# A graph network's large node update: the gain of the first norm moved from POOL to DVE's last pass over t

## The chip, the cores and the metric

The kernel runs on one core of one Trainium2 chip. The metric is the device time of one launch in microseconds, median of three runs. One profiled execution of the same program stands beside the runs. The engines are named as in the profile: PE is TensorE (PEld its weight loads), DVE is VectorE, ACT is ScalarE, POOL is GpSimd, SP is SyncE, which here only starts DMAs.

## The reference, cut to what matters

The network has four layers on 50,000 nodes of 64 channels and 25,000 edges: two message layers, one layer with attention over the edges, and a matrix exponential. The change lies in what the third layer does to every node after its attention sums are there:

```python
agg = agg @ Wo + bo
agg = agg * (1.0 + 0.5 * jnp.tanh(gamma))[None, :] + beta[None, :]
x = _layer_norm(node_embeddings + agg, ln1_g, ln1_b)
h = jax.nn.gelu(x @ W1 + b1, approximate=False) @ W2 + b2
return _layer_norm(x + h, ln2_g, ln2_b)

def _layer_norm(x, g, b, eps=1e-05):
    m = jnp.mean(x, axis=-1, keepdims=True)
    v = jnp.mean((x - m) ** 2, axis=-1, keepdims=True)
    return (x - m) * jax.lax.rsqrt(v + eps) * g + b
```

Around it x is normed without weights, clipped at zero and handed to this layer, and the layer's result is added to x; then the next norm follows, whose result the fourth layer reads.

## The kernel before, in words

`node_update` (from line 1421) runs three times, once per layer; the changed branch is `layer == 2`, called the large node update here. It takes the nodes in 14 chunks (`SUPER`) of 128 partitions x 28 rows (`G`) x 64 channels. A tile of a chunk, as `T`, `XC` or `Y`, has 1792 elements in each partition. Each chunk is worked in 7 subchunks (`SUBS`) of 4 rows. Chunks alternate between two buffers `s`. `at(t, d)` names chunk 2t + d.

For each chunk there are two phases, and the engines write out the same order. In the attend phase PE turns the gathered attention rows `A` (`turn`), ACT copies them out of PSUM, PE multiplies by `w_out`, and DVE evacuates each subchunk into T with the layer's input Z added (line 1844). In the MLP phase PE turns T, multiplies by `w1`, ACT applies the gelu with bias `b1`, PE multiplies by `w2`, and DVE evacuates each subchunk, adds it to the gained t and writes Y (line 1846). PE's product of subchunk i + 2 waits for DVE's evacuation of subchunk i, as there are two PSUM buffers. PE runs attend(d) and then mlp(d - 1), in turn.

Between the evacuations DVE works on whole chunks. After T is whole come its row sums (`total`, line 1811), the scaling of `mean` and the centring (`centre`, lines 1815 and 1817), the row sums of ACT's squares (`variance`, line 1821), ACT's root, and then `scale` (lines 1825 and 1830): the reciprocal of the deviation and one tensor_tensor that writes `xc * rstd` over T. This is DVE's last pass over t; it stands in the next chunk's attend phase behind evacuation 1 and raises `t_ready`, for which PE's MLP phase waits. In the same attend phase stand, after evacuation 0, the last pass of an older chunk into H (line 1829), after evacuation 2 the centring of Y, after evacuation 3 the addition of the last bias to X (line 1940), after evacuation 4 the addition of H to X (line 1943), and after evacuation 5 the variance of Y.

The norm's weight and bias `ln1_g` and `ln1_b` aren't applied to T. `prepare` folds them into the MLP: `b1` gets the bias through `w1`, and the rows of `w1` are multiplied by `g1`, the weight as a column (line 266). The sum t + MLP needs t times the weight as well, though; this product is POOL's. `gained` (line 2028) waits for `t_ready` and writes TG = T * `norms[:, 0]` (line 2031), and DVE's first evacuation of the MLP phase waits for `tg_ready`.

POOL's other work is `gather` (line 2033): 28 indirect DMAs for each chunk, 392 in all, each of which fetches one row of 64 channels for every partition into `A` (line 2039). A gather waits until the buffer's last user is through (`inputs_used`). The order on POOL's queue is gather 0, gather 1, and then gained(d), gather(d + 2) for every d.

SP's queue issues all loads and stores; at the start of the program it issues 41 weight loads (line 216), and all engines wait for the last of them.

Of the kernel before, what the change touches and what calls it, by code (L numbers as in the profile page):

```python
# [20 lines left out]
P = 128  # L21
NODES, EDGES, C = 50000, 25000, 64
NH, HD, NET, FF = 4, 16, 8, 128
G = 28
# [106 lines left out]
def prepare(nc, net):  # L131

    d = net.dram
    with ExitStack() as ctx:
        ctx.callback(nc.all_engine_barrier)
        def sb(name, shape, dt=F32):
            return ctx.enter_context(nc.sbuf_tensor(name, shape, dt))
# [5 lines left out]
        bf_row = sb("bf_row", [1, 2 * C])  # L143
        bo_row = sb("bo_row", [1, C])
        wo = sb("wo", [P, C])
        g1 = sb("g1", [P, 1])
        a1 = sb("a1", [C, 1])
        a1_row = sb("a1_row", [1, C])
        rows = sb("rows", [1, 4, C])
# [30 lines left out]
        with nc.Block() as block:  # L180
# [17 lines left out]
                (bf_row[:, :], d["L2_gnn_bf"][None, :]), (bo_row[:, :], d["L2_gnn_bo"][None, :]),  # L198
                (wo[0:C, :], d["L2_gnn_Wo"][:, :]), (wo[C:P, :], d["L2_gnn_Wo"][:, :]),
                (net.w1[0:C, :], d["L2_gnn_W1"][:, :]), (net.w1[C:P, :], d["L2_gnn_W1"][:, :]),  # L200
                (g1[0:C, :], d["L2_gnn_ln1_g"][:, None]), (g1[C:P, :], d["L2_gnn_ln1_g"][:, None]),
                (a1[:, :], d["L2_gnn_ln1_b"][:, None]), (a1_row[:, :], d["L2_gnn_ln1_b"][None, :]),
                (net.b1[:, :], d["L2_gnn_b1"][:, None]),
                (net.w2[:, :], d["L2_gnn_W2"][:, :]), (rows[:, 3, :], d["L2_gnn_b2"][None, :]),
# [36 lines left out]
            def _(v):  # L241
# [21 lines left out]
                nc.vector.tensor_tensor(rows[:, 3, :], rows[:, 3, :], a1_row[:, :], ALU.add)  # L263
                v.wait_ge(up_bias_done, 1)
                nc.vector.tensor_tensor(net.b1[:, :], net.b1[:, :], ps3[:, 0:1], ALU.add)
                nc.vector.tensor_scalar(net.w1[:, :], net.w1[:, :], g1[:, :], None, ALU.mult)
                v.wait_ge(spread_done, 1)
                for half in (slice(0, C), slice(C, P)):
                    nc.vector.tensor_tensor(net.w_out[half, half], wo[half, :], ps2[half, 0:C], ALU.mult)
# [1154 lines left out]
def node_update(nc, net, layer, sums=None):  # L1424
# [19 lines left out]
    with ExitStack() as ctx:  # L1444
# [48 lines left out]
            cols_loaded, rec_ready, scattered = map(sem, ("cols_loaded", "rec_ready", "scattered"))  # L1493
        if layer == 2:
            Y = [sb(f"y{s}", [P, G, C]) for s in range(2)]
            TG = [sb(f"tg{s}", [P, G, C]) for s in range(2)]
            node_end = sb("node_end", [P, SUPER, G])
            ends_loaded = sem("ends_loaded")
            u = [sb(f"u{b}", [FF, 2, CH // 2]) for b in range(2)]

            pf = [ctx.enter_context(nc.psum_tensor(f"{n}pf{b}", [P, 2, 512], F32)) for b in range(2)]
            loaded_x = [sem(f"loaded_x{s}") for s in range(2)]
            gathered = [[sem(f"gathered{s}_{i}") for i in range(SUBS)] for s in range(2)]
            up_done, gelu_done, t_ready, tg_ready, tail_ready = map(
                sem, ("up_done", "gelu_done", "t_ready", "tg_ready", "tail_ready"))
        weight = (net.w_upd, net.w_lin, net.w_out)[layer]
        x_in = (net.x_in, net.x1, net.x2)[layer]
        h_in = (net.h0, net.h1d, net.h2)[layer]
# [9 lines left out]
        def at(t, d):  # L1518

            return 2 * t + d, d % 2, t + d // 2  # L1520
# [9 lines left out]
        with nc.Block() as block:  # L1530
# [271 lines left out]
            def _(v):  # L1802
# [20 lines left out]
                def scale(y, r, n=0, relu=False):  # L1823
# [5 lines left out]
                        return nc.vector.scalar_tensor_tensor(y, XC[n][:, :, :], 0.0, spread(rstd[n][:, :]), ALU.max, ALU.mult)  # L1829
                    return nc.vector.tensor_tensor(y, XC[n][:, :, :], spread(rstd[n][:, :]), ALU.mult)  # L1830

                def evacuate(c, phase, i, m):
                    q, b, s = phase[0] * SUBS + i, (phase[1] + i) % 2, c[1]
                    rows = slice(i * J, (i + 1) * J)
                    got = po[b][:, 0:J * C].rearrange("p (j c) -> p j c", c=C)
                    v.wait_ge(mm_done, q + 1)
                    if layer == 0:
                        to = sums[:, bass.ds(G * c[0] + i * J, J), 0:C]
                        nc.vector.scalar_tensor_tensor(to, got, 0.0, X[s][:, rows, :], ALU.max, ALU.add).then_inc(evacuated, 1)
                    elif layer == 1:  # L1840
                        to = sums[:, bass.ds(G * c[0] + i * J, J), 0:C]
                        nc.vector.tensor_tensor(to, got, X[s][:, rows, :], ALU.add).then_inc(evacuated, 1)
                    elif m == 0:
                        nc.vector.tensor_tensor(T[s][:, rows, :], got, Z[s][:, rows, :], ALU.add).then_inc(evacuated, 1)
                    else:
                        nc.vector.tensor_tensor(Y[s][:, rows, :], got, TG[s][:, rows, :], ALU.add).then_inc(evacuated, 1)

                def counts(c):

# [70 lines left out]
                else:  # L1920
                    def attend(c, phase, x=None, t=None, y=None):

                        for i in range(SUBS):
                            if c is not None:
                                if i == 0:
                                    v.wait_ge(loaded[c[1]], 16 * in_loads * (c[2] + 1))
                                evacuate(c, phase, i, 0)
                            if x is not None and i == 0:
                                v.wait_ge(stored_h[x[1]], 16 * x[2])
                                nc.vector.tensor_copy(H[x[1]][:, :, C:C + 1], node_end[:, bass.ds(x[0], 1), :].rearrange("p n g -> p g n"))  # L1930
                                scale(H[x[1]][:, :, 0:C], 2 * x[0] + 1, 1, relu=True).then_inc(normed, 1)
                            elif t is not None and i == 1:
                                scale(T[t[1]][:, :, :], t[0]).then_inc(t_ready, 1)
                            elif y is not None and i == 2:
                                centre(Y[y[1]][:, :, :], 1)
                            elif y is not None and i == 5:
                                variance(2 * y[0], 1)
                            if y is not None and i == 3:
                                v.wait_ge(loaded_x[y[1]], 16 * (y[2] + 1))
                                nc.vector.tensor_tensor(X[y[1]][:, :, :], X[y[1]][:, :, :], channels(net.norms[:, 3, :]), ALU.add)  # L1940
                            elif x is not None and i == 4:
                                v.drain()
                                nc.vector.tensor_tensor(X[x[1]][:, :, :], X[x[1]][:, :, :], H[x[1]][:, :, 0:C], ALU.add).then_inc(tail_ready, 1)
                        v.drain()
                        if c is not None:
                            v.sem_inc(inputs_used, 1)

                    def mlp(c, phase, t=None, y=None):

                        for i in range(SUBS):  # L1950
                            if c is not None:
                                if i == 0:
                                    v.wait_ge(tg_ready, c[0] + 1)
                                evacuate(c, phase, i, 1)
                            if t is not None:
                                if i == 0:
# [45 lines left out]
            def _(pool):  # L2002
# [19 lines left out]
                        scatter(number)  # L2022
                    pool.wait_ge(scattered, 16 * (BLOCKS // 2))
                else:
                    def channels(which):
                        return net.norms[:, which, :].unsqueeze(1).to_broadcast([P, G, C])

                    def gained(c):

                        pool.wait_ge(t_ready, c[0] + 1)  # L2030
                        nc.gpsimd.tensor_tensor(TG[c[1]][:, :, :], T[c[1]][:, :, :], channels(0), ALU.mult).then_inc(tg_ready, 1)

                    def gather(c):
                        number, s, h = c
                        if h > 0:
# [1 line left out]
                        for j in range(G):  # L2037
                            tile = G * number + j
                            pool.indirect_dma_start(A[s][:, j, :], None, net.attended[:, :],  # L2039
                                                    bass.IndirectOffsetOnAxis(ap=net.dst_end[:, tile:tile + 1], axis=0)).then_inc(gathered[s][j // J], 16)  # L2040
                    gather(at(0, 0))
                    gather(at(0, 1))
                    for d in range(SUPER):
                        gained(at(0, d))
                        if d + 2 < SUPER:
                            gather(at(0, d + 2))


def diffuse(nc, net):
# [620 lines left out]
```

## Time and profile before

| | us |
|---|---|
| timed runs (3) | 4831.4, 4833.33, 4836.11; median 4833.33 |
| the profiled execution | 4836.01 |
| its span, first to last instruction | 4834.2 |
| PE busy | 3138.6 (65%) |
| DVE busy | 2784.6 (58%) |
| POOL busy | 2933.4 (61%) |
| ACT busy | 1030.1 (21%) |
| the large node update | about 2714 to 3536 of the span |

All times in the profile are microseconds from the start of the span, unless a row says ns. A timeline row gives start, duration, engine, line, operation, what is written and read, and the count of merged instructions; in square brackets stands how long the engine had been idle before it and what released it. The start of the next row of the same engine, not the end of a row, tells what a row costs its queue, as rows overlap a little. A row that waits for a port or a lock is shown as a long row, not as an idle time.

### The profile page before, as it was taken

The page shows a single profiled execution, that of the slowest core. Times are in us where ns is not written, and L with a number is a line of the kernel's source. Part 1 is how long each engine was busy: PE and PEld are TensorE (multiplying, and loading weights), DVE is VectorE, ACT ScalarE, POOL GpSimd, SP SyncE. Part 2 cuts the span into 40 slices and gives each one's busy share as a digit, 9 for nine tenths or more (in the row PEclk, how much of TensorE's full clock was granted, in tenths as well). Part 3 has the DMA queues.
Part 4 walks back from the last instruction along what each step waited for, and adds up shares of the span by engine and source line. Part 5 has one row for each costly group of instructions (what it writes and reads, how often), then busy time and mean ns, then how long its engine had stood idle before and what let it go on. Part 6 is the DMA issues. An engine that isn't in the chain of part 4 may idle for free. (4 is left out here: it accounts for less than half of the span.)

```text
span 4834.2 us, 57222 instructions
## 1 busy us (share of the span) xinstructions
PE 3138.6 (65%) x11768; PEld 1938.3 (40%) x11768; DVE 2784.6 (58%) x6520; ACT 1030.1 (21%) x1952; POOL 2933.4 (61%) x2538
## 2 busy tenths in 40 slices
PE   2746776668977886647777477777636665555424
PEld 1533444446766774432222255555412222222113
DVE  4746787864552223657777358887755555444323
ACT  1410222222221111212222133333312211111100
POOL 0048888404548835867777588777137776887631
PEclk7655566665555555555555555555568887766755
DMA  2636222214541103531222424334111111233215
GB/s 102 269 128 202 68 58 58 49 47 126 154 134 24 24 10 117 185 136 41 42 41 42 65 51 94 79 81 98 50 52 38 36 38 32 30 30 30 23 14 109
DMA packets 337304, 363.44 MB, mean 75 GB/s; under 512 B 238020, under 2 KB 269518, under 8 KB 337152
## 3 DMA queue, kind: packets, MB, share of 16 engines
q1 hardware_dynamic: 223040, 262.47, 16.8%
q0 software_dynamic: 94096, 80.75, 12.9%
q10 hardware_dynamic: 20016, 18.41, 1.1%
q8 instruction: 68, 1.11, 0.1%
q14 instruction: 84, 0.69, 0.0%
HBM read 213.54 MB, written 189.07 MB: 83 GB/s over the span
## 5 line engine op out<-in xcount | busy, mean ns | idle before, releaser
L1119 PE MATMUL e_ps<-e_msg,e_hot 128*128 x2408 | 528.8, 398 | 251.1 <-issue 119.3
L1119 PEld LDWEIGHTS e_ps<-e_msg,e_hot 128*128 128x128 f32 x2408 | 492.8, 302 | 324.7 <-issue 318.6
L2039 POOL DMA_INDIRECT u_a<-attended,dst_end x392 | 487.4, 1243 | 146.5 <-issue 116.3
L2389 PE MATMUL d_pl<-d_hot,d_fields 128*65 128x512 f32 x712 | 481.7, 839 | 0.0
L845 POOL DMA_INDIRECT e_msg<-from_src,e_src x200 | 208.9, 1044 | 354.8 <-DMA e_first<-lot_first 300.4
L2333 POOL DMA_INDIRECT flows<-d_out,d_end x160 | 264.3, 1652 | 106.3 <-issue 101.3
L959 DVE TENSOR_TENSOR e_ps<-e_ps,e_before 128x65 f32<-128x65 f32 (+1 forms) x172 | 39.6, 230 | 469.1 <-PE e_ps L1119 469.1
L2008 POOL DMA_INDIRECT list<-u_rec,place x200 | 263.9, 1320 | 56.8 <-issue 56.2
L2320 POOL DMA_INDIRECT d_near<-term,d_rec x196 | 189.9, 969 | 156.4 <-DMA d_rec<-list 97.0
L1717 ACT ACTIVATE u_zt<-u_pt 128x256 f32<-128x256 f32 (+1 forms) x392 | 162.8, 431 | 534.0 <-PE u_pt L1617 509.8
L1222 POOL DMA_INDIRECT a_ends<-h,a_src x200 | 211.8, 1059 | 90.8 <-issue 60.1
L898 ACT ACTIVATE sums<-e_ps 128x455 f32 (+1 forms) x172 | 94.0, 547 | 791.1 <-DVE e_ps L959 791.1
L1623 PE MATMUL u_po<-bias_parts,ones 3*128 3x256 bf16 x392 | 148.8, 379 | 160.3 <-ACT u_zt L1717 78.9
L850 POOL DMA_INDIRECT e_msg<-h1d,e_src x200 | 196.5, 983 | 88.9 <-issue 54.0
L2328 POOL DMA_INDIRECT flows<-d_out,d_end x196 | 205.7, 1050 | 68.5 <-issue 57.2
L2389 PEld LDWEIGHTS d_pl<-d_hot,d_fields 128*65 128x65 f32 x712 | 134.1, 202 | 276.7 <-issue 276.7
L847 POOL DMA_INDIRECT e_near<-from_dst,e_dst x200 | 205.5, 1027 | 61.0 <-issue 61.0
L2381 PE MATMUL d_pr<-ident,d_scan 65*128 65x65 f32 x356 | 62.2, 317 | 273.7 <-DVE d_scan L2499 273.7
L1222 POOL DMA_INDIRECT a_ends<-h,a_dst x200 | 196.1, 981 | 66.0 <-issue 66.0
L2320 POOL DMA_INDIRECT d_near<-terms,d_rec_idx x168 | 163.4, 973 | 102.6 <-DMA d_rec_w<-list_w 53.8
L2016 POOL TENSOR_TENSOR u_z<-sums,u_inv_count 128x1792 f32<-128x1792 f32 x14 | 44.6, 3184 | 290.1 <-DVE u_rec L1912 181.3
L2370 PE MATMUL d_pc<-d_liveb,d_before 128*128 128x4 bf16 x89 | 14.7, 165 | 307.6 <-DVE d_prod L2476 307.4
(361 smaller groups left out, 7912.0 us busy)
## 6 DMA issues: line engine op xcount, KB each, us to landing
u_z<-h SPq DMA_DIRECT2D x28, 896.0 KB, 6.5
x<-sums SPq DMA_DIRECT2D x28, 896.0 KB, 7.8
u_x<-x SPq DMA_DIRECT2D x28, 896.0 KB, 7.9
terms<-zero_rows SPq DMA_DIRECT2D x16, 812.5 KB
e_key_row<-src_key SPq DMA_DIRECT2D x50, 256.0 KB
h1d<-u_h SPq DMA_DIRECT2D x14, 910.0 KB, 9.5
u_z<-h1d SPq DMA_DIRECT2D x14, 910.0 KB, 4.7
term<-u_h SPq DMA_DIRECT2D x14, 910.0 KB, 3.7
```

What stands on the lines that cost most here:

```text
L845: pool.indirect_dma_start(msg[:, b, 0:C], None, net.from_src[:, :], bass.IndirectOffsetOnAxis(ap=src[:, b:b + 1], axis=0)).then_inc(gather ...
L847: pool.indirect_dma_start(near[c % 3][:, j, :], None, net.from_dst[:, :], bass.IndirectOffsetOnAxis(ap=dst[:, b:b + 1], axis=0)).then_inc( ...
L850: pool.indirect_dma_start(msg[:, b, :], None, net.h1d[:, :], bass.IndirectOffsetOnAxis(ap=src[:, b:b + 1], axis=0)).then_inc(gathered[c % ...
L1119: last = nc.tensor.matmul(to, hot[s][:, q, :], rows, start=False, stop=q == LOT - 1)
L1222: pool.indirect_dma_start(ends[s][:, j, half * C:(half + 1) * C], None, net.h2[:, :], bass.IndirectOffsetOnAxis(ap=rows, axis=0)).then_inc ...
L1717: nc.scalar.activation(zt[b][:, :], pt[b][:, 0:TURNS * P], ACT.Copy).then_inc(zt_ready, 1)
L2008: pool.indirect_dma_start(net.lists0[:, :], bass.IndirectOffsetOnAxis(ap=at_place, axis=0), rec[:, t, :], None).then_inc(scattered, 16)
L2039: pool.indirect_dma_start(A[s][:, j, :], None, net.attended[:, :], bass.IndirectOffsetOnAxis(ap=net.dst_end[:, tile:tile + 1], axis=0)).th ...
L2320: pool.indirect_dma_start(near[s][:, j, :], None, table[:, :], bass.IndirectOffsetOnAxis(ap=row, axis=0)).then_inc(gathered[s], 16)
L2328: pool.indirect_dma_start(net.flows[:, :], bass.IndirectOffsetOnAxis(ap=end[s][:, j:j + 1], axis=0), out[s][:, j, 0:C], None, bounds_check ...
L2333: pool.indirect_dma_start(net.flows[:, :], bass.IndirectOffsetOnAxis(ap=end[s][:, j:j + 1], axis=0), out[s][:, j, 0:C], None, bounds_check ...
L2389: last = nc.tensor.matmul(pl[0:WEIGHT + 1, :], fields[:, j, :], hot[:, j, :], start=j == 0, stop=j == J - 1)
```

## The change

- DVE's last pass over T becomes a helper of its own, `gained`: after the reciprocal it issues 28 scalar_tensor_tensor instructions, one for each row j of the chunk, on 64 elements per partition: T[j] = XC[j] * rstd[j] * `norms[:, 0]`. The deviation is the per-partition scalar operand. The last of them raises `t_ready`.
- T now holds the gained t, so the MLP's evacuation adds T itself. TG, its product on POOL, the semaphore `tg_ready` and DVE's wait for it are gone.
- As the turned T carries the weight already, `prepare` no longer multiplies `w1` by it; the tile `g1`, its two loads and that one instruction go.
- POOL's queue has only the gathers, 0 to 13, each behind its own wait for the buffer.

```diff
-        g1 = sb("g1", [P, 1])
...
-                (g1[0:C, :], d["L2_gnn_ln1_g"][:, None]), (g1[C:P, :], d["L2_gnn_ln1_g"][:, None]),
...
-                nc.vector.tensor_scalar(net.w1[:, :], net.w1[:, :], g1[:, :], None, ALU.mult)
...
-            TG = [sb(f"tg{s}", [P, G, C]) for s in range(2)]
...
+                def gained(c):
+
+                    v.wait_ge(rstd_ready[0], c[0] + 1)
+                    nc.vector.reciprocal(rstd[0][:, :], rstd[0][:, :])
+                    v.drain()
+                    for j in range(G):
+                        last = nc.vector.scalar_tensor_tensor(T[c[1]][:, j, :], XC[0][:, j, :], rstd[0][:, j:j + 1], net.norms[:, 0, :], ALU.mult, ALU.mult)
+                    last.then_inc(t_ready, 1)
...
-                        nc.vector.tensor_tensor(Y[s][:, rows, :], got, TG[s][:, rows, :], ALU.add).then_inc(evacuated, 1)
+                        nc.vector.tensor_tensor(Y[s][:, rows, :], got, T[s][:, rows, :], ALU.add).then_inc(evacuated, 1)
...
-                                scale(T[t[1]][:, :, :], t[0]).then_inc(t_ready, 1)
+                                gained(t)
...
-                                if i == 0:
-                                    v.wait_ge(tg_ready, c[0] + 1)
...
-                    def gained(c):
-
-                        pool.wait_ge(t_ready, c[0] + 1)
-                        nc.gpsimd.tensor_tensor(TG[c[1]][:, :, :], T[c[1]][:, :, :], channels(0), ALU.mult).then_inc(tg_ready, 1)
-
...
-                    gather(at(0, 0))
-                    gather(at(0, 1))
                     for d in range(SUPER):
-                        gained(at(0, d))
-                        if d + 2 < SUPER:
-                            gather(at(0, d + 2))
+                        gather(at(0, d))
```

## Rows read from the trace of the kernel before

**Rows 1.** The page's first part: busy time, share of the span and instructions of each engine.
```profile
PE 3138.6 (65%) x11768; PEld 1938.3 (40%) x11768; DVE 2784.6 (58%) x6520; ACT 1030.1 (21%) x1952; POOL 2933.4 (61%) x2538
```

**Rows 2.** Windows of one step: from:to, length, busy (count) of each engine, PE clock, DMA.
```profile
3073.00:3125.80 52.80, 40.87 (x155) 28.57 (x155) 42.19 (x38) 17.54 (x29) 39.80 (x30) 0.50 0.39 87
```

**Rows 3.** Timeline of one attend phase in the steady part.
```profile
3089.70 2.03 DVE L1830 TENSOR_TENSOR u_t<-u_xc,u_rstd 128x1792 f32<-128x1792 f32 x1
3091.64 0.42 DVE L1844 TENSOR_TENSOR u_t<-u_po,u_z 128x256 f32<-128x256 f32 x1
3091.81 3.96 POOL L2031 TENSOR_TENSOR u_tg<-u_t,norms 128x1792 f32<-128x1792 f32 x1 [4.62 <-DVE u_t L1830]
3092.16 3.65 DVE L1815 TENSOR_SCALAR u_mean<-u_mean 128x28 f32<-128x28 f32 x1
3095.88 2.09 DVE L1817 TENSOR_TENSOR u_xc<-u_y,u_mean 128x1792 f32<-128x1792 f32 x1
3097.90 0.41 DVE L1844 TENSOR_TENSOR u_t<-u_po,u_z 128x256 f32<-128x256 f32 x1
3098.41 0.37 PE L1623 MATMUL u_po<-bias_parts,ones 3*128 3x256 bf16 x1 [4.20 <-issue]
3101.98 1.06 PE L1617 MATMUL u_pt<-ident,u_t 128*128 128x128 f32 x4
```

**Rows 4.** Timeline: gathers beside DVE's work; a small operation's min/median/max ns.
```profile
3060.52 2.03 DVE L1830 TENSOR_TENSOR u_y<-u_xc,u_rstd 128x1792 f32<-128x1792 f32 x1
3060.99 2.38 POOL L2039 DMA_INDIRECT u_a<-attended,dst_end  x1 [0.30 <-issue]
3062.98 0.39 DVE L1815 TENSOR_SCALAR u_mean<-u_mean 128x28 f32<-128x28 f32 x1
...
L2464 DVE TENSOR_TENSOR d_keep<-d_srcs x89: 161/163/213, 3561.3 to 4698.8; 128x4 bf16<-128x4 f32 x89
```

**Rows 5.** Timeline, DVE: back to back operations with a per-row scalar.
```profile
560.53 0.34 DVE L1015 SCALAR_TENSOR_TENSOR e_unread<-e_key_row,e_key,e_earlier 128x128 bf16<-128x128 f32 x1
560.79 0.48 DVE L1015 SCALAR_TENSOR_TENSOR e_unread<-e_key_row,e_key,e_earlier 128x256 bf16<-128x256 f32 x1
561.36 0.62 DVE L1015 SCALAR_TENSOR_TENSOR e_unread<-e_key_row,e_key,e_earlier 128x384 bf16<-128x384 f32 x1
561.90 0.75 DVE L1015 SCALAR_TENSOR_TENSOR e_unread<-e_key_row,e_key,e_earlier 128x512 bf16<-128x512 f32 x1
...
3569.02 0.22 DVE L2490 SCALAR_TENSOR_TENSOR d_slot<-d_upto,d_ahead,d_live 128x4 f32<-128x4 f32 x1
3569.16 0.28 DVE L2491 TENSOR_SCALAR d_place<-d_upto,d_ahead,d_passed 128x4 f32<-128x4 f32 x1
```

**Rows 6.** 64 elements: fours back to back (busy us, mean ns), and lone ones (min/median/max ns).
```profile
L1393 DVE TENSOR_TENSOR a_out<-a_sums,a_dsum 128x64 f32<-128x64 f32 x200 | 30.8, 216 | 6.0 <-issue 4.1
...
L2557 DVE SCALAR_TENSOR_TENSOR d_total<-d_pr,d_tail_coef,d_total x35: 283/283/285, 4740.9 to 4813.4; 128x64 f32<-128x64 f32 x35
```

**Rows 7.** Timeline, third and fourth attend phase; the scalings, 2904 to 3434 and 2860 to 3400.
```profile
2834.39 0.66 PE L1617 MATMUL u_pt<-ident,u_a 128*128 128x128 f32 x2 [5.27 <-DMA u_a<-attended,dst_end]
2836.56 0.42 DVE L1844 TENSOR_TENSOR u_t<-u_po,u_z 128x256 f32<-128x256 f32 x1 [4.82 <-PE u_po L1643]
...
2881.71 6.45 DVE L1940 TENSOR_TENSOR u_x<-u_x,norms 128x1792 f32<-128x1792 f32 x1
...
L1815 DVE TENSOR_SCALAR u_mean<-u_mean x31: 179/392/4424, 2903.8 to 3432.6; 128x28 f32<-128x28 f32 x31
...
L1815 DVE TENSOR_SCALAR u_mean<-u_mean 128x28 f32<-128x28 f32 x31 | 39.9, 1288 | 2.9
```

**Rows 8.** Timeline behind the last chunk's attend phase.
```profile
3460.43 3.98 DVE L1815 TENSOR_SCALAR u_mean<-u_mean 128x28 f32<-128x28 f32 x1
```

**Rows 9.** Timeline of the preparation: the two loads of g, DVE's scaling of w.
```profile
17.36 1.24 SPq L216 DMA_DIRECT2D g<-in_L_gnn_ln_g  x2
...
28.08 0.27 DVE L266 TENSOR_SCALAR w<-w,g 128x128 f32<-128x128 f32 x1
```

More of the change, by code:

```diff
@@ L1503, in node_update @@
             gathered = [[sem(f"gathered{s}_{i}") for i in range(SUBS)] for s in range(2)]
-            up_done, gelu_done, t_ready, tg_ready, tail_ready = map(
-                sem, ("up_done", "gelu_done", "t_ready", "tg_ready", "tail_ready"))
+            up_done, gelu_done, t_ready, tail_ready = map(
+                sem, ("up_done", "gelu_done", "t_ready", "tail_ready"))
         weight = (net.w_upd, net.w_lin, net.w_out)[layer]
@@ L2024, in _ @@
                 else:
-                    def channels(which):
-                        return net.norms[:, which, :].unsqueeze(1).to_broadcast([P, G, C])
-                    def gained(c):
-                        pool.wait_ge(t_ready, c[0] + 1)
-                        nc.gpsimd.tensor_tensor(TG[c[1]][:, :, :], T[c[1]][:, :, :], channels(0), ALU.mult).then_inc(tg_ready, 1)
                     def gather(c):
```

## The prediction

> **What bounds the kernel now.** I read the page's line of busy times first. No engine is busy for more than 65% of the span [rows 1], so there is no one bound, and the place to look is the stage itself. The windows of the large node update show a steady step of 52.8 us per chunk, the same from window to window, with TensorE granted 0.50 (its 1.2 GHz level), DVE busy for 42.2 of 52.8 us and POOL for 39.8 [rows 2]. The timeline of one step then shows who sets its end [rows 3]. In the attend phase DVE runs without an idle bracket from the evacuation at 3091.64 on; TensorE sits idle 4.20 us until 3098.41 and then starts right behind DVE's evacuation of 3097.90, which ends at 3098.31. So in this phase DVE's queue is the path, one for one. In it stands one strange row: the 28-element `mean` scaling at 3092.16 takes 3.65 us. Elsewhere the same line takes 0.39 [rows 4]. It starts 0.35 us after POOL's product (3091.81, 3.96 us) and ends with it, at 3095.8: POOL's product holds DVE.
>
> POOL itself is not the path. Its queue waits 4.62 us for t before the product [rows 3], and what I found of TensorE waiting long for gathers lies in the first attend phases, as the 5.27 us at 2834.39 [rows 7].
>
> **The change part by part.**
>
> (a) *DVE's pass over t.* It was one instruction whose next one starts 1.94 us later (3089.70 to 3091.64) [rows 3]. It becomes 28 instructions of 64 elements, each with a per-row scalar and a second tensor from SBUF. The nearest row is a scalar_tensor_tensor of the same kind at four lengths, in the edge stage [rows 5]. Start to next start is 0.26 us for 128 elements (560.53 to 560.79) and 0.54 for 384 (561.36 to 561.90): 0.28 us for 256 more, 1.09 ns each; DVE's full passes, 2.03 us for 1792 less the fixed part, give 1.05. At 1.05 what is left is 0.13 and 0.14 us. A 4-element one with a per-row scalar and no accumulator is followed after 0.14 us, which says the same [rows 5]. So 64 elements cost 0.067 + 0.135 = 0.20 us each, 28 of them 5.6 us: +3.66 us per chunk over 1.94. The ends: without per-row scalars fours of 64 elements are busy 30.8/50 = 0.616 us, of which the last takes its whole 0.216, so one follows another after (0.616 - 0.216)/3 = 0.133 us, 3.7 us in all; if nothing overlaps, each takes the whole 0.283 us of a lone one of this form and length, 7.9 us [rows 6]. I take 0.20, as the form with the scalar operand is measured and the others differ in it or in being alone.
>
> A rule speaks against the change. The Trainium skill ("VectorE: DVE Perf Modes", the section on the TRN2 errata) says that SBUF-source operations pay a fixed latency for each instruction, so that many small tiles pay it many times and one should use 512 elements or more. Its formula (N + 151)/0.96 ns would give 0.224 us for 64 elements, an estimate of 6.3 us for the 28 and some 0.7 us more per chunk than my term. The rows agree with the rule's kind and with less than its size: 0.135 us between starts beside the elements, where the formula has 0.157.
>
> (b) *The stall.* From the start of the `mean` scaling to the start of the centring behind it were 3092.16 to 3095.88 = 3.72 us, and the centring itself took 0.08 longer than its neighbours (2.02 to the next start, not 1.94) [rows 3]. Without the product the scaling takes 0.39 us beside a gather [rows 4] and 0.18 alone, the least of its group [rows 7], 0.08 more to the next start: 0.26 to 0.47. Gain 3.54 us, or 3.33 if a gather stands in the way as in rows 4. The two together: +3.66 - 3.54 = +0.12 us per chunk, up to +0.33. What was a stall becomes work of the same length. Evacuation 3 would start at 3098.0 to 3098.2 where it started at 3097.90.
>
> What is late next: evacuation 2 moves from 3091.64 to 3095.3, so the TensorE products that wait for it come 3.6 us later. They hide in the 4.20 us that TensorE now idles before 3098.41 and are done (1.22 us) before evacuation 3. The signal that t is ready comes at 3095.3; TensorE asks for it first after the last attend product, at 3101.98 [rows 3], so 6 us of cover are left.
>
> (c) *Beside gathers.* DVE's two-input operations begun while a gather runs are not held: the one at 3060.52 took its usual 2.03 us though a gather ran until 3060.69 (the next one's start less its 0.30 of idle). The gather that starts behind it is held, 2.38 us. The 28 row operations are of that kind. A small two-input operation that runs beside other gathers takes 163 ns in the median and 213 at most, 0.05 more [rows 4]; with 4 gathers a pass 0 to +0.2 us a chunk; I take 0.1.
>
> (d) *Which chunks.* The product stalls DVE at the `mean` scaling in 10 attend phases (the fourth chunk's to the last's); in 9 of them by about 3.65 us, in the first by 4.42 (nine of the ten lie in the window whose 31 scalings sum to 39.9 us: 4.4 + 8 x 3.65 + 22 short ones of 0.29 in the mean) [rows 7]. Nine chunks at +0.12 + 0.1 = +2.0 us; the first of them, whose stall was 0.77 longer, -0.5. One phase earlier the same product holds the bias addition, 6.45 us where 2.0 are usual [rows 7]: 3.66 - 4.44 = -0.8. One before that the product holds nobody, but TensorE waits 5.27 us for the last gather. Those gathers stood behind one product of 4.0 us and now come that much earlier, so with DVE's +3.66 the phase is DVE's and no longer the gather's. Evacuation 5, now at 2836.56 after 4.82 us of idle, finds DVE free at 2831.74 + 3.66 = 2835.4 [rows 7]: -1.1. In the first such phase DVE waits for gathers anyway: 0. After the last chunk's attend phase the scaling loses 3.98 - 0.18 = 3.8 us [rows 8] and the pass gains 3.6: -0.2. Sum of the stage: 2.0 - 0.5 - 0.8 - 1.1 - 0.2 = -0.6 us.
>
> (e) *POOL's queue.* It loses 14 products and 14 waits and issues the same 392 gathers. Each gather of a chunk may now start when its buffer is free (the end of the attend phase two chunks before) and not behind the product; POOL gets up to 44 us ahead of need. Nothing waits for it in the steady part, so this is worth nothing there.
>
> (f) *Preparation.* Two loads of `g` go from SP's queue: 1.24 us and the step to the next, -1.3 us, all on the path, since every engine there waits for the last load; and the scaling of `w` on DVE goes, 0.27 us long and 0.2 to the next start [rows 9]. If the loads' landing and not their issue set the end, it would be 0 instead of -1.3.
>
> Sum: -0.6 - 1.3 - 0.2 = -2.1 us on the profiled execution's 4836.0. The three timed runs have their median at 4833.3, 2.7 us lower; I put the forecast against the median: 4831.2, rounded to 4831.5 us.
>
> **How steep it is.** 12 chunks and the tail make 13 x 28 = 364 row operations on the path. Each 0.01 us of error in their pitch is 3.6 us. My reading of the rows is good to 0.01. A measurement can tell about 0.2% from no change, 9.7 us: that takes a pitch below 0.18 or above 0.232.
>
> **The rivals.**
>
> *A. The row operations follow each other faster, 0.133 us.* For it: the form without a per-row scalar does so [rows 6]. Against: the rows with a scalar show 0.135 us of fixed cost beside the elements [rows 5], and this would leave 0.07. Then 364 x 0.067 = 24 us less, though part ends where TensorE's 1.9 us a sub-chunk takes over: 4808 to 4815 us, say 4811. The Trainium skill ("Vector Engine (DVE) Microarchitecture Reference", Measured stream behaviour on trn2) states about 75 ns per instruction after queue overlap; by that the estimate is 0.142 us each, which is this case. The form without scalars agrees with it, the form with one does not.
>
> *B. Slower: the row operations do not overlap, or each gather that begins holds one.* Place: DVE's queue between evacuations 1 and 2. Price: at the 0.283 us of a lone one, 364 x 0.083 = +30 us: 4862; at half of that 4846. It decides from a pitch of 0.232 on. For it: 28 in a row, all reading the same `norms` row and a scalar, are nowhere in the trace, and gathers run beside them. Against: rows 5 were measured overlapping, and rows 4 show DVE unheld. The Trainium skill ("SBUF — State Buffer", Who interferes with whom) says that of a two-input DVE operation and a POOL instruction that reads SBUF, whoever is first holds the port for its whole instruction; a gather of 0.94 us first in line would then cost more than 0.05. The trace agrees for POOL's product and for gathers begun behind DVE, and not for DVE begun behind a gather.
>
> *C. The `mean` scaling falls behind a gather.* It is held by one already (0.39 for 0.18 us [rows 4]); with POOL no longer in step with DVE it may meet the start of one and wait up to 0.9 us: 10 x 0.5 = +5 us: 4836.5, still no change.
>
> **How the numbers follow.** The forecast 0.72, C 0.07, A 0.09, B 0.12. Within 0.2% are the first two, nearly whole: 0.78. Faster: A and the low edge of the first, 0.11. Slower: B without its mildest part, 0.11. The range takes the forecast's own error (364 x 0.01, some 3 us of gathers, 3 us of runs), C, and of B and A the near part: 4821 to 4845.
>
> **What would show it.** On DVE between evacuation 1 and 2 of a steady chunk 28 rows that fill 5.6 us; the `mean` scaling behind them 0.2 to 0.4 us; steps of 52.8 to 53.1 us; TensorE's gap moved from before evacuation 3 to before evacuation 2; POOL without products, idle some 8 us a step. Wrong would be a pass under 5.0 or over 6.4 us, a `mean` scaling over 1 us, or TensorE waiting for gathers in the steady part.

## The result, and the profile after

The changed kernel takes 4842.11 us (median of 20 runs, 4837.59 to 4845.91), the kernel before beside it 4836.41 (20 runs, 4827.73 to 4843.71). The ratio is 1.0014 with a 95% interval of 1.0007 to 1.0020: slower by 5.7 us, a small but certain loss. The forecast was no change, with a sum of -2.1 us. The time lies within the range; the direction is wrong. Each profile below is one execution; the two kernels' profiled executions took 4836.01 and 4843.38 us.

At the place of the change the trace of the changed kernel shows what was forecast. First the attend phase that answers to [rows 3], DVE alone, and the window of its step beside [rows 2]:

```profile
3084.34 0.42 DVE L1849 TENSOR_TENSOR u_t<-u_po,u_z 128x256 f32<-128x256 f32 x1
3084.67 0.32 DVE L1831 RECIPROCAL u_rstd<-u_rstd 128x28 f32<-128x28 f32 x1
3085.07 5.72 DVE L1834 SCALAR_TENSOR_TENSOR u_t<-u_xc,u_rstd,norms 128x64 f32<-128x64 f32 x28
3090.71 0.41 DVE L1849 TENSOR_TENSOR u_t<-u_po,u_z 128x256 f32<-128x256 f32 x1
3091.22 0.18 DVE L1811 TENSOR_SCALAR u_mean<-u_mean 128x28 f32<-128x28 f32 x1
3091.47 2.02 DVE L1813 TENSOR_TENSOR u_xc<-u_y,u_mean 128x1792 f32<-128x1792 f32 x1
3093.41 0.42 DVE L1849 TENSOR_TENSOR u_t<-u_po,u_z 128x256 f32<-128x256 f32 x1
```

```profile
3071.50:3124.50 53.00, 40.94 (x156) 28.59 (x154) 42.38 (x66) 17.54 (x29) 33.95 (x29) 0.50 0.38 87
```

The 28 row operations fill 3085.07 to 3090.71 = 5.64 us, a pitch of 0.20. The scaling behind them is down from 3.65 to 0.18 us. The step is 53.0 us where it was 52.8, and POOL is busy for 33.95 us of it where it was 39.80. PE's gap has moved ahead of evacuation 2, as its row shows:

```profile
3091.23 0.37 PE L1619 MATMUL u_po<-bias_parts,ones 3*128 3x256 bf16 x1 [3.57 <-issue]
```

The preparation is shorter too: DVE's first copy behind the last weight load starts at 24.37 us; it started at 25.92 in the kernel before.

```profile
24.37 0.23 DVE L246 CAST identb<-ident 128x128 bf16<-128x128 f32 x1 [23.10 <-DMA norms<-in_L_gnn_ln_b]
```

So the loss must be elsewhere. I laid the two traces beside each other, stage by stage. At the start of the last stage, `diffuse` (the matrix exponential; none of its lines are changed), the changed kernel is 3.98 us ahead: DVE's copy of the first coefficient starts at 3550.87 against 3554.85. At the stage's end, DVE's copy of `d_tail_out`, it is 7.4 us behind: 4822.95 against 4815.55. The last stage takes 1272.1 us for 1260.7: 11.4 us are lost in code that nobody touched. The lead of 3.98 us at its start is only in part the change's doing: 1.55 us arise in the preparation, the large node update takes 0.3 us more, and 2.7 us arise between the two, nearly all in stages without a changed line. Over the thirteen profiled executions of this document that stretch takes 2701.3 to 2709.2 us. DVE's timeline shows where. This is the hand-over between two steps of the exponential, where the DVE program's step loop jumps back, in the kernel before:

```profile
4489.01 0.15 DVE L2523 COPY d_have<-d_passed 128x1 f32<-128x1 f32 x1 [8.99 <-DMA list_w<-d_kept]
...
4489.34 0.06 DVE L2527 MEMSET d_passed<- 128x1 f32 x1
4490.02 0.15 DVE L2515 COPY d_coef<-d_ratios 128x1 f32 x1 [0.62 <-issue]
...
4605.71 0.15 DVE L2515 COPY d_coef<-d_ratios 128x1 f32 x1 [0.61 <-issue]
```

and in the changed one:

```profile
4486.65 0.15 DVE L2514 COPY d_have<-d_passed 128x1 f32<-128x1 f32 x1 [10.96 <-DMA list_w<-d_kept]
...
4486.99 0.06 DVE L2518 MEMSET d_passed<- 128x1 f32 x1
4490.40 0.15 DVE L2506 COPY d_coef<-d_ratios 128x1 f32 x1 [3.36 <-issue]
...
4610.35 0.15 DVE L2506 COPY d_coef<-d_ratios 128x1 f32 x1 [3.11 <-issue]
...
4671.71 0.15 DVE L2506 COPY d_coef<-d_ratios 128x1 f32 x1 [3.33 <-issue]
```

The copy waits for no semaphore ("issue"), yet it comes 3.1 to 3.4 us after the last instruction instead of 0.6, three times. The loop makes four passes with two steps in each, so three is the number of its jumps back; at the step in the middle of a pass the wait stays 0.18 us in both. Together 2.74 + 2.50 + 2.71 = 7.95 us. The DMA view of the last stage has one more difference, in the queue that carries instructions. Columns: kind, packets, MB, share. Before, then after:

```profile
q14 instruction: 21, 0.17, 0.0%
```

```profile
q14 instruction: 37, 0.30, 0.1%
```

16 packets and 0.13 MB more. They fall on the waits. Between 4400 and 4700 us of the span the kernel before has no packet on this queue and the changed one has 14. Two of them begin in the first wait and two in the third; of the second wait's pair one begins 0.5 us ahead of it and one in it. This is the row for 4487.0 to 4490.4 us of the changed kernel, the first wait:

```profile
q14 instruction: 2, 0.02, 1.9%
```

An engine that sits idle without a wait, at a jump back, while code is fetched: the suspicion is the length of DVE's program. Counted in the built programs, DVE has 157 instructions more in front of the last stage. The node update's pass over t is written out at six places and each has 27 more, 162 in all; four waits for `tg_ready` and the scaling of `w1` are gone. The step loop of 302 instructions starts at instruction 3160 before and at 3317 after.

### The profile page after: what moved, and what is told of

Its sections match the earlier page's. It is cut to its first block and busy times, and to the rows that moved or that the text cites. A ratio compares the mean times of both kernels' runs of the same rounds, so it can differ in the third digit from the quotient of the medians.

```text
span 4841.6 us, 57577 instructions
## 1 busy us (share of the span) xinstructions
PE 3121.5 (64%) x11768; PEld 1934.1 (40%) x11768; DVE 2794.0 (58%) x6897; ACT 1029.7 (21%) x1952; POOL 2859.9 (59%) x2524
## 5 line engine op out<-in xcount | busy, mean ns | idle before, releaser
L2034 POOL DMA_INDIRECT u_a<-attended,dst_end x392 | 466.8, 1191 | 207.2 <-issue 117.3
```

## Experiments: is it the place of the code?

Theory 1: the loop's place in the program decides, as its jumps back have to fetch code. Rivals: the row operations or the missing product themselves hurt the last stage; or any longer program costs, in proportion to its length.

**157 idle instructions in the kernel before.**

```diff
+                    for j in range(156):
+                        nc.vector.memset(T[0][:, j // C, j % C:j % C + 1], 0.0)
+                    v.drain()
                     v.wait_ge(ends_loaded, 16)
```

> The kernel before, with 156 one-column memsets of tile T and one drain put into DVE's program of the last node update, ahead of its wait for the first attended rows (DVE idles 26.7 us there). DVE's program then has as many instructions ahead of the last stage's step loop as the changed kernel (3317 ahead of the loop's first, against 3160), and nothing else of the change is in it. Theory 1 (the 5.7 us that the change lost are code: the step loop of 302 instructions, which starts at 3317, touches three blocks of 256 instead of two, and its three jumps back have to fetch code): the idle time ahead of the d_coef copies at the third, fifth and seventh repeat grows from 0.62 to about 3.3 us as in the changed kernel, queue 14 carries some 16 packets more in the last stage, and the time rises by 8 to 11 us over the kernel before, to about 4846. Theory 2 (the row operations or the missing product cost it, directly or by what they leave behind for the last stage): no change, within 1 us of before, the copies wait 0.62. Theory 3 (any longer program of DVE costs fetches in proportion to its length): the loss is there, but a pad of 100 costs two thirds of it.

Measured 4844.35 us (6 runs) beside 4831.44 (22 runs): ratio 1.0030 (1.0018 to 1.0042). The loss, and by the medians more than all of it (the two intervals overlap), comes from 157 instructions of no meaning. The last stage takes 1269.8 us. A row of DVE's timeline and the whole run's instruction queue:

```profile
4491.41 0.15 DVE L2518 COPY d_coef<-d_ratios 128x1 f32 x1 [3.13 <-issue]
```

```profile
q14 instruction: 101, 0.83, 0.1%
```

The kernel before has 84 packets on this queue in the whole run, the changed one 101. The node update is untouched by the pad: its steps are 52.81 us. That rules out the rival in which the row operations are to blame.

**100 of them.** The same with `range(99)`.

> The same with 99 memsets and a drain: the step loop starts at 3260 and its 302 instructions end at 3562, inside two blocks of 256 (3072 to 3583). Theory 1: no loss, the d_coef copies wait 0.62 us, the time within 1 us of before. Theory 3 (length alone): two thirds of the loss of the pad of 157, 5 to 7 us. Theory 2: no change.

Measured 4830.84 us (11 runs) beside the same 4831.44: ratio 1.0004 (0.9995 to 1.0013). No loss at two thirds of the length:

```profile
4483.52 0.15 DVE L2518 COPY d_coef<-d_ratios 128x1 f32 x1 [0.60 <-issue]
```

So it is not length alone. It is the place.

**30 more in the changed kernel**, at the same place in the node update (`range(29)` and the drain).

> The changed kernel with 29 memsets and a drain more in DVE's program at the same place, which puts the step loop's start from 3317 to 3347, past the block boundary at 3328, and its end to 3649, before 3840. Theory 1: a longer program is faster: the copies wait 0.62 us again, the last stage loses its 8 to 11 us, and the kernel comes out at 4831 to 4835, 8 to 11 us under the changed one and 1 to 5 under the one before (the forecast's sum was -2). Theory 2: no change, 4842. Theory 3: the same or up to 2 us slower.

Measured 4834.42 us (11 runs) beside 4831.44: ratio 1.0006 (0.9997 to 1.0015), no longer slower with certainty. A longer program gave the last stage its time back (1261.7 us, waits of 0.59, 0.57 and 0.57). It came out 3 us above the kernel before and not under it, and the node update has part of the reason: with the pad ahead of it, every second of its steps took 53.3 to 53.5 us, where the changed kernel's take 53.0 to 53.2. So I moved the pad.

**The 30 at the start of the last stage.**

```diff
                 nc.vector.memset(fields[:, :, :], 0.0)
+                for j in range(29):
+                    nc.vector.memset(hot[:, 0, j:j + 1], 0.0)
+                v.drain()
                 v.wait_ge(loaded, 6 * 16)
```

> The changed kernel with the 30 small instructions at the start of the last stage, ahead of DVE's wait for its constants (4.5 us idle), instead of in the node update: the node update's code lies exactly as in the changed kernel, only the step loop moves to 3347. Code theory: d_coef copies wait 0.6 us, the last stage takes 1260 us, the node update's steps are 52.99 us without the alternating 53.3 of the run with the pad ahead of the node update, and the time is that of the change with its code effect gone: by the forecast's sum 2 us under the kernel before (4829 to 4835), against 3 over it in the run with the pad in the node update. A theory in which it is the place of the node update's own code that counts: no change, 4842.

Measured 4831.37 us (11 runs) beside 4834.40 (15 runs): ratio 0.9993 (0.9984 to 1.0002). The steps are those of the changed kernel (53.5 to 52.8 us, none alternating), the last stage takes 1260.9 us, and the row at the jump back is short again:

```profile
4486.01 0.15 DVE L2509 COPY d_coef<-d_ratios 128x1 f32 x1 [0.59 <-issue]
```

No packet of queue 14 falls on the jumps back. This is the change as the forecast had priced it, without its effect on the last stage: -3.0 us, where the sum said -2.1. The interval, some -7.7 to +1.0 us, holds no change as well.

**Where the boundary lies.** One execution each, with 11 and with 20 instructions in the node update.

> The changed kernel with 11 small instructions instead of 30: the step loop's first instruction is then number 3328, exactly 13 x 256. One look, for where the boundary lies. Code theory with no shift between the written instructions and the fetched blocks: the d_coef copies of the third, fifth and seventh repeat wait 0.6 us and queue 14 carries about 84 packets. If a few instructions stand ahead that the program doesn't show, also 0.6; if the blocks begin earlier (a negative shift), 3.3 us and about 101 packets.

> The changed kernel with 20 small instructions in the node update: the step loop starts at 3337, between 3328 (still slow: copies waiting 3.1 to 3.3 us) and 3347 (0.57 us). One look, to place the boundary: 0.6 us if it lies 1 to 9 instructions later than counted, 3.2 us if 10 to 19.

Both still wait. With 11 the loop starts at 3328, where the expectation without a shift had the boundary; it lies later. Here are the rows of the first jump, with 11 and then with 20.

```profile
4490.30 0.15 DVE L2509 COPY d_coef<-d_ratios 128x1 f32 x1 [3.16 <-issue]
```

```profile
4487.01 0.15 DVE L2509 COPY d_coef<-d_ratios 128x1 f32 x1 [3.14 <-issue]
```

All placements in one table. The last stage is counted from DVE's first `d_coef` copy to its `d_tail_out` copy.

| kernel | loop starts at | idle at the three jumps, us | queue 14, packets | last stage, us |
|---|---|---|---|---|
| before | 3160 | 0.62 0.61 0.62 | 84 | 1260.7 |
| before + 100 | 3260 | 0.60 0.59 0.58 | 84 | 1259.9 |
| changed | 3317 | 3.36 3.11 3.33 | 101 | 1272.1 |
| before + 157 | 3317 | 3.13 3.34 3.19 | 101 | 1269.8 |
| changed + 11 | 3328 | 3.16 3.27 3.09 | 101 | 1270.1 |
| changed + 20 | 3337 | 3.14 3.06 3.05 | 101 | 1266.7 |
| changed + 30 | 3347 | 0.59 0.57 0.57 | 86 | 1261.7 |
| changed + 30, last stage | 3347 | 0.59 0.57 0.57 | 86 | 1260.9 |

The slow band begins above 3260 and ends between 3337 and 3347. The Trainium skill ("Runtime: NRT & Kernel Launch", Instruction fetch mechanics) says that the instruction memory of most engines holds two blocks of 16 KiB, 256 instructions each, and that a taken branch to a target outside this window forces a fetch. The table and the packets in the waits agree with it; the size of a block is the Trainium skill's, as no run here measures it. What follows is an estimate from it. A loop of 302 instructions fits into two blocks of 256 in most places; it touches three when more than 512 - 302 = 210 instructions of its first block lie ahead of it, which are 45 of 256 places. The end of the band, 3338 to 3347, would be such a block's start, 10 to 19 instructions later than counted, for a reason that stays open; then the band is the 45 places below it, and 3260 lies outside and 3317 to 3337 inside. The lower edge was not tried. The Trainium skill gives no time for the fetch; here it is 2.5 to 2.7 us at each jump back. The four executions with long waits average 1269.7 us in the last stage. Eight with short waits (four of the table and one of each of the four kernels below) lie from 1258.5 to 1264.3 and average 1261.4. So the effect is 8.3 us, and the added idle time at the three jumps, 7.4 to 8.0 us, is nearly all of it. The 11.4 us of the first pair are this effect and a difference between single executions.

## Experiments: the two terms, and a better version

**The product alone taken away** (the last addition takes t, the weight is left out of the residual).

> The kernel before without POOL's product t x norm weight and the wait for it; the last addition takes t itself, so the norm weight is left out of the residual, and nothing else differs (DVE's pass stays one instruction). It measures step (b) alone. By the forecast the scaling of the mean no longer stalls: -3.5 us a chunk, steps of 49.3 instead of 52.8 us, about -40 us in all: 4790 to 4797. The rival, that another wait takes over (gathers or PE become the bound at once): steps of 50.5 to 52.8 and a time above 4805; steps of 52.8 if the product's stall was not on the path at all.

```diff
-                        nc.vector.tensor_tensor(Y[s][:, rows, :], got, TG[s][:, rows, :], ALU.add).then_inc(evacuated, 1)
+                        nc.vector.tensor_tensor(Y[s][:, rows, :], got, T[s][:, rows, :], ALU.add).then_inc(evacuated, 1)
...
-                                if i == 0:
-                                    v.wait_ge(tg_ready, c[0] + 1)
...
-                        gained(at(0, d))
```

Measured 4788.81 us (4 runs) beside 4834.87 (7 runs): ratio 0.9905 (0.9889 to 0.9922), 1 us under what was expected. Steps of 49.49 us, 3.32 less than 52.81. That is the forecast's smaller value for the stall, 3.33, the one with a gather in the way, and DVE's row shows that gather's mark:

```profile
3069.98 0.40 DVE L1815 TENSOR_SCALAR u_mean<-u_mean 128x28 f32<-128x28 f32 x1
```

**The row operations alone** (POOL's product stays, so the weight is multiplied in twice; not shown in the cut are 29 memsets and a drain, which keep the last stage's loop out of the slow band).

> The kernel before with DVE's pass made as 28 row operations as in the change, while POOL's product, its wait and w1's scaling stay (the norm weight is multiplied in twice); 30 small instructions ahead of it keep the last stage's step loop (start 3352, end 3654) within two blocks. It measures step (a) alone. By the forecast the whole 3.7 us of each chunk lie on the path and the stall behind POOL stays: steps of 56.4 to 56.5, +40 to +48 us, 4872 to 4880. The rival, that part of the pass was hidden (the change's near zero was the difference of two smaller numbers): steps under 55.5. The last stage keeps its 1260 us and the waits of 0.6 us at the jumps back by the code theory; by a theory in which row operations hurt the last stage it takes 1270.

```diff
-                                scale(T[t[1]][:, :, :], t[0]).then_inc(t_ready, 1)
+                                v.wait_ge(rstd_ready[0], t[0] + 1)
+                                nc.vector.reciprocal(rstd[0][:, :], rstd[0][:, :])
+                                v.drain()
+                                for j in range(G):
+                                    last = nc.vector.scalar_tensor_tensor(T[t[1]][:, j, :], XC[0][:, j, :], rstd[0][:, j:j + 1], net.norms[:, 0, :], ALU.mult, ALU.mult)
+                                last.then_inc(t_ready, 1)
```

Measured 4879.6 us (4 runs) beside 4834.87: ratio 1.0092 (1.0075 to 1.0109), +45 us. The steps alternate between 56.37 and 56.69 us, +3.7 in the mean, and the stall behind POOL is still there:

```profile
3101.47 5.57 DVE L1937 SCALAR_TENSOR_TENSOR u_t<-u_xc,u_rstd,norms 128x64 f32<-128x64 f32 x28
3106.97 0.41 DVE L1844 TENSOR_TENSOR u_t<-u_po,u_z 128x256 f32<-128x256 f32 x1
3107.47 3.65 DVE L1815 TENSOR_SCALAR u_mean<-u_mean 128x28 f32<-128x28 f32 x1
```

So the near zero was a true difference: a gain of about 46 us and a loss of 45. The last stage has its short waits of 0.59 and 0.57 us here, with all the row operations in the program (the loop starts at 3352).

**Two whole passes instead of 28 rows**, in the changed kernel.

> The changed kernel with the 28 row operations replaced by two passes of the whole chunk (deviation, then norm weight) with a drain between: about 3.9 us instead of 5.64 per chunk, by the pass of 1.94 us in the kernel before, and 150 instructions fewer ahead of the last stage, so that the step loop lies in two blocks again. Theory 1 with the forecast's sum for the node update: -1.7 us x 12 chunks = -20 us in the node update and the 8 to 11 us of the last stage back: 4812 to 4816. Theory 2: if the missing product, not the row operations, hurt the last stage, only the -20: 4822. If the pass is not on the path that sets the step after all: 4831 to 4834 by theory 1.

```diff
-                    for j in range(G):
-                        last = nc.vector.scalar_tensor_tensor(T[c[1]][:, j, :], XC[0][:, j, :], rstd[0][:, j:j + 1], net.norms[:, 0, :], ALU.mult, ALU.mult)
-                    last.then_inc(t_ready, 1)
+                    t = T[c[1]][:, :, :]
+                    nc.vector.tensor_tensor(t, XC[0][:, :, :], spread(rstd[0][:, :]), ALU.mult)
+                    v.drain()
+                    nc.vector.tensor_tensor(t, t, channels(net.norms[:, 0, :]), ALU.mult).then_inc(t_ready, 1)
```

Measured 4813.53 us (5 runs) beside 4831.44 (22 runs): ratio 0.9959 (0.9945 to 0.9972), faster than both. The two passes, with the drain between them, take 3079.74 to 3083.78 = 4.04 us:

```profile
3079.74 2.02 DVE L1834 TENSOR_TENSOR u_t<-u_xc,u_rstd 128x1792 f32<-128x1792 f32 x1
3081.84 2.03 DVE L1836 TENSOR_TENSOR u_t<-u_t,norms 128x1792 f32<-128x1792 f32 x1
3083.78 0.42 DVE L1850 TENSOR_TENSOR u_t<-u_po,u_z 128x256 f32<-128x256 f32 x1
3084.30 0.39 DVE L1811 TENSOR_SCALAR u_mean<-u_mean 128x28 f32<-128x28 f32 x1
```

The steps are 51.6 us, 1.35 under the changed kernel's: 1.6 us from the pass, less 0.2 as the scaling meets a gather again.

**The product on DVE where DVE idles.** POOL's product goes from the kernel before, DVE's pass stays one instruction, and the product is made ahead of the first addition that needs it. DVE idles there in the kernel before, in a steady chunk:

```profile
3110.67 0.42 DVE L1846 TENSOR_TENSOR u_y<-u_po,u_tg 128x256 f32<-128x256 f32 x1 [5.39 <-PE u_po L1669]
```

```diff
                                 if i == 0:
-                                    v.wait_ge(tg_ready, c[0] + 1)
+                                    nc.vector.tensor_tensor(TG[c[1]][:, :, :], T[c[1]][:, :, :], channels(net.norms[:, 0, :]), ALU.mult)
+                                    v.drain()
...
-                        gained(at(0, d))
```

> The kernel before with the product t x norm weight moved from POOL to DVE, as one pass of about 2 us (by DVE's passes of the same shape) just ahead of the first addition of the second product, where DVE idles 5.46 us for PE. DVE's pass over t stays one instruction of 1.94 us, POOL only gathers. By the forecast's parts the stall of 3.54 us goes, no row operation is added, and the new pass fits in the idle time: as without the product, steps of 49.3 to 49.6, 4791 to 4799, faster than both kernels by 35 to 50 us. The rival, that the 5.46 us are not free because the evacuations behind them come late: steps 2 us longer than without the product, 4815 to 4825. By the code theory the last stage keeps 1260 us (its loop starts at 3167).

Measured 4790.21 us (4 runs) beside 4834.87: ratio 0.9909 (0.9893 to 0.9926). A second time, with other kernels beside it:

> The kernel that makes the product on DVE ahead of the first addition, once more beside the others of this call: 4788 to 4794 where the kernel before takes 4831 to 4836, ratio 0.990 to 0.992.

4786.43 us (4 runs) beside 4834.40 (15 runs): 0.9901 (0.9886 to 0.9916). DVE's rows show the product in the idle time, 3.24 us of which are left behind it:

```profile
3076.09 2.02 DVE L1953 TENSOR_TENSOR u_tg<-u_t,norms 128x1792 f32<-128x1792 f32 x1
3081.36 0.42 DVE L1846 TENSOR_TENSOR u_y<-u_po,u_tg 128x256 f32<-128x256 f32 x1 [3.24 <-PE u_po L1669]
```

The step is 49.49 us, the same as without any product, so the product is free there. Both times the kernel came out 1 to 2 us under the range expected:

```profile
3062.98:3112.47 49.49, 41.08 (x157) 28.67 (x158) 40.90 (x40) 17.55 (x29) 40.96 (x29) 0.51 0.41 93
```

This version beats both kernels by about 1%. Its step loop starts at 3168 (six places with two instructions more, four waits fewer), not 3167 as the expectation has it, outside the slow band; its waits are 0.62 us.

## Why the prediction was right or wrong

(a) The pass: 5.6 us forecast, 5.64 measured (pitch 0.20 us, 392 operations of 269 to 354 ns, overlapped). The sum was made from operations at four lengths with the same per-row scalar, not from the faster form without one and not from a lone one. That choice was right; rivals A and B, which priced the pitch otherwise, fell. Alone it costs +3.7 us a step.

(b) The stall: 3.54 or 3.33 us forecast, 3.32 measured alone. In the changed kernel the scaling has a median of 180 ns, its smallest value; with one pass in front of it, it takes 0.40. The longer row of operations has moved it off the gather. Rival C, which had it fall behind one, was wrong in the steady part:

```profile
L1811 DVE TENSOR_SCALAR u_mean<-u_mean x30: 179/180/393, 2912.2 to 3428.9; 128x28 f32<-128x28 f32 x30
```

(b, c) Together +0.22 us a steady chunk forecast. Between first evacuations the sixth and seventh interval measured +0.35 and +0.34, the next five +0.17 to +0.20, the last -0.03. With the fifth, -0.42 (53.58 to 53.16), the nine make +1.15 us where 2.0 - 0.5 = 1.5 were said.

(d) The early chunks in the same way: the third interval -1.37 (51.40 to 50.03; forecast -1.1), the fourth -0.50 (53.99 to 53.49; forecast -0.8). The tail from the last chunk's first evacuation to the last stage is 151.76 and 151.55: -0.2 as forecast. The second interval, set by the gathers, is 55.3 to 55.6 us in the kernel before and its two padded versions, and between 53.1 and 56.7 in the changed one and its four; the forecast of 0 there is neither confirmed nor refuted by these executions.

Over the whole stage, from its first evacuation to the last stage, the pair gives +0.3 us (820.5 to 820.8) where the sum said -0.6; that is mostly the second interval.

(e) POOL's queue: worth nothing in the steady part, as forecast. The idle time was read too small, though. The prediction has POOL idle some 8 us a step; it is busy for 33.95 of 53.0 us, 19 idle, and by [rows 2] it was idle for 13 before.

(f) The preparation: the two loads were put at -1.3 us, and DVE's first copy comes 1.55 us earlier (25.92 to 24.37). The other profiled runs have 25.6 with the two loads and 24.4 to 24.7 without, so 0.9 to 1.3 us is the likelier figure. The scaling of `w`, put at -0.2, is worth 0.15: DVE's next pass, over `w_out`, starts 1.70 us earlier.

The step that failed is in (a), and it is the one that no term of the sum stands for: "It becomes 28 instructions". I priced the 28 where they run, at 3.66 us a chunk, and not what they do to the program around them. They are written out at six places and push DVE's later code by 157 instructions; the last stage's loop got into a place where each jump back fetches code, which costs 8.3 us. No term of the sum and no rival had it. By the Trainium skill's block size 45 of 256 places are of this kind, an estimated chance of about 1 in 6 for a loop whose place nobody chose.

With this one effect undone the change measured -3.0 us for a forecast of -2.1, both no change within what can be measured. The mechanism at the changed place was right, but that the two numbers lie so near each other is partly luck: single terms missed by up to 0.4 us in both directions, and the second interval alone differs by up to 3.6 us between the changed kernel and its padded versions.

The other thing that was too coarse is the limit of 9.7 us below which the prediction says that nothing can be told from no change. With 20 runs of each kernel 5.7 us were told from it, so a loss of this size needed a chance of its own.

No row of the kernel before shows the danger, as its waits at the jump back are 0.6 us. What would have warned me is the count: 3160 plus 157, set beside the loop's 302 instructions and the Trainium skill's blocks of 256.

The prediction's arithmetic also held the better kernel: it says that the stall is worth 3.54 us a chunk and that the pass costs 3.66, but stops at their difference. Whoever asks for the first without the second finds DVE's 5.39 us of idle time ahead of the addition.

## What to carry to other kernels

When an edit changes how many instructions an engine's program holds, look for loops of between one and two blocks (here 302 instructions) behind it on the same engine, in stages that the edit doesn't touch, and compare the idle time at their jumps back and the instruction queue's packets in both traces. A pad of idle instructions, placed where the engine waits anyway, tells such an effect from a real one, and can take it away. It has to be long enough: here 30 did it, 11 and 20 did not. And where a sum is a large gain less a large price, test each alone: here the gain could be had without the price.

## What the hardware showed that was not expected

- A jump back of DVE's program can cost 3.1 to 3.4 us instead of 0.6, by the loop's place alone. The row shows it as idle time with no wait, and queue 14 carries 15 to 17 packets of 8 KB more than in the kernels with short waits. In the changed kernel each of the three passes behind a slow jump has five of them, two of these during the wait or just ahead of it.
- Instructions ahead of the large node update's own loop have a small effect too: in the changed kernel with 30 ahead of it every second step is 0.3 us longer (53.3 for 52.98); with 11 or 20 ahead, or with the 30 behind it, it is not so in the last steps. The kernel with the row operations alone, which has 30 ahead as well, alternates in the same way (56.69 for 56.37), but was not run without them, and the one with two passes alternates by 0.12 with none. Why is open.
- A small DVE operation behind 28 row operations met no gather in the median (180 ns), and behind one or two whole passes it did (0.39 to 0.40 us), though POOL issues the same gathers. Which of two streams is in step with the other can be worth 0.2 us a step.
